# Front end of a fused attention and gated feed-forward kernel: four first projections split at once, value projections moved ahead, first scores in the first slot

## The chip, the cores and the metric

One core of one Trainium2 chip runs the whole program. The metric is the device time of one execution in microseconds (us); lower is better. TensorE (PE) does the matmuls, VectorE (DVE), ScalarE (ACT) and GpSimd (POOL) the elementwise work, and SyncE (SP) issues all the DMA transfers.

## What is computed

Input x is 2 x 1024 tokens of 512 features. The reference, cut to what matters:

```
xn = layernorm(x)                                   # over 512 features
q  = xn @ Wq            -> 32 heads of 16
kv = xn @ Wkv           -> 8 groups, a key and a value of 16 each (4 heads share a group)
w  = softmax(causal(q k^T) / 4);  ctx = w v;  s = ctx @ Wo + bo
gate, up = xn @ gate_w^T + lora,  xn @ up_w^T + lora        # 1376 hidden
g  = silu( (silu(gate) * up) @ down_w^T + lora )
out = x + s * g
```

## The kernel before

**Chunks.** The 2048 tokens are cut in four chunks `c` of 512. For each chunk the kernel normalises x (`layernorm`, DVE; its square root is `root`, ACT), transposes it on PE (`turn_x`, 4 turns a chunk, tile `ring` to a PSUM bank), rounds it (`round_x`, `x_hi`), copies it (`copy_x`, `xT`) and makes the rest (`low_x`, `x_lo`). Products in nearly full precision are three matmuls with high and low parts (L246 to L248). A projection `("proj", c, blk)` is 4 steps of three 512-column matmuls; block 4 (`KEYS_BLOCK`) makes the keys of all groups, blocks 0 to 3 make the queries of eight heads each. Its result is split in a high part on ACT (`split_projection`, L1125) and a low part on DVE (`low_projection`, L1374), and SP stores three pieces of it in DRAM (`store_projection`, L618, tiles `scratch_q` and `scratch_k`). A value `("value", c, 0)` is 4 steps of four 128-column matmuls (L896); ACT copies it (`copy_value`, L1132, tile `v_sb`, two buffers) and SP stores it (`store_value`, L623). The projections are counted by `projection(c, blk)`: 0 to 3 are `LEADING` (keys and block 0 of chunks 0 and 1), 4 is (0,1), 5 the keys of chunk 2, 6 is (1,1), 7 the keys of chunk 3.

**Two programs in one.** Each engine interleaves a background (all the projections, then the feed-forward) with the attention. `interleave` first runs `LEAD` steps of the background alone. Then it goes slot by slot: 40 slots are a round, round -1 comes first, then 16 rounds, one for each pair of a group and a batch. The `EARLY` steps are spread over round -1, and one background step falls to each slot of the rounds 0 to 15. PE, SP and POOL run their attention one slot further on than the others (`background_first` is false).

**Scores.** In round i the attention of pair i (scores transposed `st`, L1054; exponential, L1297; context, L1071) runs beside the maxima of pair i+1: 48 units, each a score matmul `s` (L1035, two units to a pair of matmuls) with a maximum on DVE (L1516 with the diagonal, L1519 without) through three PSUM banks. `stream_slots` spreads the pairs of units over the slots by their widths. The first 16 units of a pair need only the first 512 tokens, the other 32 all of them. SP loads q and k for them: for the first pair in two parts (`load_first`, L600 and L602, which waits at L598 until projections 0 and 1 lie in DRAM; then L790 and L793 at slot 1 of round -1, which wait at L785 for projections 2 and 3). For the second pair all comes at slot 1 of round 0 (again L790 and L793), after a wait at L785 until projections 6 and 7 lie in DRAM. PE's first score matmuls of the second pair stand in slot 6 of round 0; they are the 64x128 pair in front of the second turn of the maxima (L1042).

**The low-rank factors.** `split_low_b` (ACT, L1138) and `low_of_low` (DVE, L1380) prepare tile `bT`; `split_low_a` (L1144) and the same helper prepare `low_a`, which the first `fold` on PE needs. `low_a` lies where chunk data lay, so `split_low_a` waits until all four values are stored and landed.

Of the kernel before, what the change touches and what calls it, by code (L numbers as in the profile page):

```python
# [80 lines left out]
LOAD, LOAD_V = 1, 19  # L81
FIRST_UNIT, UNIT_SLOTS = 6, 39
CONTEXT = 2
COPY_O = [15, 3]
# [38 lines left out]
def bank_order():  # L123

    for c in range(2):
        for k in range(KT):
            yield "turn", c, k
    for c, blk in LEADING:
        yield "proj", c, blk
    for c in range(2):  # L130
        yield "value", c, 0
    for c in BESIDE:
        for k in range(KT):
            yield "turn", c, k
        yield ("proj", *BESIDE[c])
        yield "proj", c, KEYS_BLOCK
        yield "value", c, 0
    for c, blk in AFTER[:SOON]:
        yield "proj", c, blk
    for i in range(2):  # L140
        yield "fold", 0, i
    for h in range(NH):
        for c in range(NCH):
            yield "hidden", h, c
            if c == 1:
                if h + 1 < NH:
                    for i in range(2):
                        yield "fold", h + 1, i
                yield "proj", *AFTER[SOON + h]
    for h in range(NH):  # L150
        yield "down_fold", h, 0
    for t in range(NT):
        yield "down", t, 0
        if 1 <= t <= NT // 2:
            yield "out", t - 1, 0
    for t in range(NT // 2, NT):
        yield "out", t, 0
# [5 lines left out]
TOTAL = sum(STEPS[kind] for kind, *_ in NUMBER)  # L163
LEAD = sum(STEPS[kind] for (kind, *_), u in NUMBER.items() if u <= NUMBER["proj", 1, 0])
EARLY = NUMBER_STEPS["fold", 0, 1] - FIRST_HIDDEN - LEAD
# [54 lines left out]
def stream_slots():  # L220
# [5 lines left out]
    for kind, n in STREAM:  # L226
        if kind == "unit" and n % 2 == 0:
            g, w = divmod(n, NU)
            even = SLOTS * g + FIRST_UNIT + UNIT_SLOTS * sum(weight[:w]) // sum(weight)
            even -= even % 2  # L230
            slot = even if even > slot else even + 1
        slots.append(slot)
# [18 lines left out]
def layer(nc, x, Wq, Wkv, Wo, bo, gate_w, up_w, down_w, low_a, low_b, low_a_down, low_b_down, out):  # L251
# [5 lines left out]
    with ExitStack() as ctx:  # L257
# [329 lines left out]
        def _(sp):  # L587
# [106 lines left out]
            def background():  # L694
# [11 lines left out]
                for c in BESIDE:  # L706
                    yield KT * STEPS["turn"]
                    for n in range(4 * (c - 2), 4 * (c - 2) + 4):
                        load_raw(n)
                    yield STEPS["proj"]  # L710
                    store_projection(*BESIDE[c])
                    yield STEPS["proj"]
                    store_projection(c, KEYS_BLOCK)
                    yield STEPS["value"]
                    store_value(c)
                for c, blk in AFTER[:SOON]:
# [139 lines left out]
        def _(pe):  # L856
# [122 lines left out]
            def background():  # L979
# [8 lines left out]
                for c in BESIDE:  # L988
                    for kt in range(KT):
                        yield from turn_x(c, kt)  # L990
                    yield from project(*BESIDE[c])
                    yield from project(c, KEYS_BLOCK)
                    yield from value(c)
                for c, blk in AFTER[:SOON]:
# [102 lines left out]
        def _(act):  # L1097
# [42 lines left out]
            def split_low_a():  # L1140
                for i in range(2):
                    act.wait_ge(v_stored[i], DMA * NCH // 2)
                act.wait_ge(xn_ready, NCH)
                nc.scalar.activation(a_gu[:, :, :], a_raw, ACT.Copy).then_inc(low_hi, 1)  # L1144
# [8 lines left out]
            def split_weight(h, i):  # L1153
                key = ("fold", h, i)
                hp = rows[h]
                wait_filled(act, key)
                nc.scalar.activation(wh[:, h % 2, i, :, 0:hp],
# [42 lines left out]
            def background():  # L1200
# [14 lines left out]
                for c, blk in LEADING:  # L1215
                    if c == 1 and blk == KEYS_BLOCK:
                        root(3)
                        split_low_b()
                        for kt in range(KT):
                            copy_x(1, kt)  # L1220
                    yield STEPS["proj"]
                    split_projection(c, blk)
                for blk in range(1, NBLK - 1):
                    round_query_weights(blk)
# [3 lines left out]
                for c in BESIDE:  # L1228
                    for kt in range(KT):
                        yield STEPS["turn"]  # L1230
                        round_x(c, kt)
                        copy_x(c, kt)
                    yield STEPS["proj"]
                    split_projection(*BESIDE[c])
                    yield STEPS["proj"]
                    split_projection(c, KEYS_BLOCK)
                    yield STEPS["value"]
                    copy_value(c)
                split_low_a()
# [92 lines left out]
        def _(dve):  # L1332
# [108 lines left out]
            def background():  # L1441
# [7 lines left out]
                for c, blk in LEADING:  # L1449
                    yield STEPS["proj"]  # L1450
                    low_projection(c, blk)
                    if (c, blk) == (0, 0):
                        layernorm(3)
                low_of_low(0, bT, b_raw, slice(2 * BESIDE_ROWS, 3 * BESIDE_ROWS))
                yield 2 * STEPS["value"]
                for c in BESIDE:
                    yield KT * STEPS["turn"]
                    yield STEPS["proj"]
                    low_projection(*BESIDE[c])
                    yield STEPS["proj"]  # L1460
                    low_projection(c, KEYS_BLOCK)
                    yield STEPS["value"]
                low_of_low(1, a_gu, a_raw, slice(BESIDE_ROWS, 2 * BESIDE_ROWS))
# [127 lines left out]
```

## Time and profile before

| | us |
|---|---|
| time, median of three runs | 984.64 (982.81 to 989.12) |
| the profiled execution's own time | 989.02 |
| its span | 987.3 |
| PE busy | 927.0 (94% of the span) |
| DVE, ACT, POOL busy | 576.7, 487.5, 318.1 |
| PE's share of the chain that ended last | 84% |
| mean granted TensorE clock | 0.977 |

The page's chain of work that ended last is followed back from the last instruction; PE holds most of it, so a moment in which PE waits is a moment of the total. All that the change touches runs in the first 110 us of the span.

### The profile page before, as it was taken

The numbers are of one execution on the slowest core, as the hardware profiler recorded it, in microseconds if no ns is written. First come the engines' busy times: TensorE is split into PE (matmuls) and PEld (weight loads), VectorE is DVE, ScalarE is ACT, GpSimd is POOL, SyncE is SP. The second block draws the span as 40 slices with busy tenths as digits, with TensorE's granted clock in tenths as the row PEclk, the third lists the DMA queues.
The fourth block names the chain that finished last, engine by engine and source line by source line (L and its number), as shares of the span: only waits on it lengthen the run. The fifth ranks groups of instructions, "written<-read, shape, count | busy, mean of one in ns | idle before, by whom it ended". The sixth has DMA issues, their size and how long they took to land.

```text
span 987.3 us, 18068 instructions
## 1 busy us (share of the span) xinstructions
PE 927.0 (94%) x6599; PEld 598.5 (61%) x6599; DVE 576.7 (58%) x1659; ACT 487.5 (49%) x978; POOL 318.1 (32%) x320
## 2 busy tenths in 40 slices
PE   2797999999999999999999999999999999999986
PEld 2665667676766676767676766554555555555764
DVE  6755666666666666666666666676566656530025
ACT  2432556565656565656565656555444434435211
POOL 4022234343535352525252525330213122120126
PEclk9899999999999999999999999989999999999998
DMA  9456242424242424242424243367565454534454
GB/s 293 132 186 206 64 136 80 133 83 134 82 134 83 133 83 125 86 124 88 119 89 124 93 127 101 101 186 195 166 169 146 124 158 122 139 105 135 144 150 150
DMA packets 142934, 129.02 MB, mean 131 GB/s; under 512 B 36176, under 2 KB 104368, under 8 KB 142624
## 3 DMA queue, kind: packets, MB, share of 16 engines
q1 hardware_dynamic: 142848, 127.87, 43.6%
q8 instruction: 54, 0.88, 0.4%
q14 instruction: 32, 0.26, 0.1%
HBM read 74.07 MB, written 53.22 MB: 129 GB/s over the span
## 4 chain that ended last, share of the span: by engine, by line
PE 84%; DVE 8%; ACT 3%; DMA 2%; issue 2%; POOL 0%; SPq 0%; POOLq 0%; DVEq 0%; ACTq 0%
PE bank L934 24%; PE o L1071 12%; PE bank L246 9%; PE s L1035 9%; PE st L1054 9%; PE bank L247 7%; PE bank L248 7%; DVE junk L1516 2%; PE bank L896 2%; DVE neg_pad L1532 1%; PE bank L909 1%; PE bank L913 1%; DVE hid L1406 1%; DMA inv_sums<-scratch_r 1%; ACT gate L1168 1%
## 5 line engine op out<-in xcount | busy, mean ns | idle before, releaser
L1297 ACT ACTIVATE prob<-st 128x512 f32<-128x512 f32 (+1 forms) x640 | 324.3, 554 | 287.7 <-PE st L1054 287.1
L1516 DVE CUSTOM_DVE_ANT_0 junk<-s,mask 128x128 bf16<-128x128 f32 (+3 forms) x512 | 229.3, 487 | 116.3 <-PE s L1035 115.5
L1519 DVE TENSOR_REDUCE part_max<-s 128x1 f32<-128x512 f32 x256 | 163.8, 681 | 103.9 <-PE s L1035 103.7
L503 POOL TENSOR_SCALAR_AFFINE_SELECT prob<-prob 128x512 f32<-128x512 f32 x128 | 82.3, 655 | 262.1 <-ACT prob L1297 261.6
L1035 PE MATMUL s<-k,q 64*128 64x512 f32 (+3 forms) x768 | 150.0, 379 | 10.5 <-DVE part_max L1516 8.5
L934 PE MATMUL bank<-x_hi,w_hi 64*128 64x512 f32 (+1 forms) x704 | 150.9, 415 | 2.4 <-DVE hid L1406 1.1
L1071 PE MATMUL o<-prob,v 128*32 128x512 f32 (+3 forms) x1536 | 145.3, 497 | 0.0
L934 PE MATMUL bank<-x_lo,w_hi 64*128 64x512 f32 (+1 forms) x704 | 142.9, 391 | 0.0
L934 PE MATMUL bank<-x_hi,w_lo 64*128 64x512 f32 (+1 forms) x704 | 142.2, 389 | 0.0
L1054 PE MATMUL st<-q,k 64*128 64x512 f32 (+3 forms) x768 | 137.2, 375 | 3.9 <-ACT prob L1297 3.8
L512 POOL TENSOR_TENSOR tanh<-tanh,hid 128x512 f32<-128x512 f32 (+1 forms) x44 | 56.5, 1285 | 166.4 <-DVE hid L1406 166.4
L1035 PEld LDWEIGHTS s<-k,q 64*128 64x128 f32 x768 | 77.3, 186 | 52.6 <-DVE part_max L1516 28.3
L1054 PEld LDWEIGHTS st<-q,k 64*128 64x128 f32 x768 | 72.0, 185 | 59.6 <-issue 35.5
L934 PEld LDWEIGHTS bank<-x_hi,w_hi 64*128 64x128 f32 (+1 forms) x704 | 68.7, 182 | 41.3 <-issue 30.6
L246 PE MATMUL bank<-down_hi,hid_in 128*128 128x512 f32 (+1 forms) x176 | 79.2, 450 | 3.0 <-issue 2.3
L520 POOL TENSOR_TENSOR hid_lo<-hid,tanh_hid_hi 128x512 fp32r<-128x512 f32 (+1 forms) x44 | 56.7, 1288 | 75.9 <-ACT tanh_hid_hi L1185 75.9
L1071 PEld LDWEIGHTS o<-prob,v 128*32 128x32 f32 x1536 | 39.7, 110 | 66.2 <-issue 62.3
L934 PEld LDWEIGHTS bank<-x_lo,w_hi 64*128 64x128 f32 (+1 forms) x704 | 69.0, 182 | 12.6
L934 PEld LDWEIGHTS bank<-x_hi,w_lo 64*128 64x128 f32 (+1 forms) x704 | 69.1, 183 | 7.4
L247 PE MATMUL bank<-down_lo,hid_in 128*128 128x512 f32 (+1 forms) x176 | 70.1, 399 | 0.0
L248 PE MATMUL bank<-down_hi,hid_in 128*128 128x512 f32 (+1 forms) x176 | 69.9, 397 | 0.0
L514 POOL TENSOR_TENSOR hid<-tanh,hid 128x512 f32<-128x512 f32 (+1 forms) x44 | 56.5, 1283 | 3.5
(121 smaller groups left out, 1014.6 us busy)
## 6 DMA issues: line engine op xcount, KB each, us to landing
hid_in<-scratch_hid SPq DMA_DIRECT2D x16, 1408.0 KB, 7.4
q<-scratch_q SPq DMA_DIRECT2D x60, 200.0 KB
scratch_hid<-tanh_hid_hi SPq DMA_DIRECT2D x40, 256.0 KB, 2.1
scratch_hid<-hid_lo SPq DMA_DIRECT2D x40, 256.0 KB, 2.4
scratch_o<-o_sb SPq DMA_DIRECT2D x32, 256.0 KB
scratch_q<-proj_hi SPq DMA_DIRECT2D x30, 256.0 KB
k<-scratch_k SPq DMA_DIRECT2D x30, 192.0 KB
ctx<-scratch_o SPq DMA_DIRECT2D x16, 256.0 KB, 3.9
```

What stands on the lines that cost most here:

```text
L246: pe.matmul(out, lhs_hi, rhs_hi, start=start, stop=False)
L247: pe.matmul(out, lhs_hi, rhs_lo, start=False, stop=False)
L248: return pe.matmul(out, lhs_lo, rhs_hi, start=False, stop=stop)
L503: ins = pool.affine_select(out=blk, in_=blk, compare_op=ALU.is_ge, fill=0.0, base=0, pattern=[[0, REP], [1, P]], channel_multiplier=-1)
L520: pool.tensor_tensor(hid_l[0:hp, n % 2], hid[0:hp, n % 2], hid_h[0:hp, n % 2], ALU.subtract)\
L934: mm = pe.matmul(bank[i][0:hp, :], w_[half, h % 2, i, kt, 0:hp], x_[half, c, kt], start=not cross and kt == 0 and w_ is wh and x_ is xh, s ...
L1035: pe.matmul(sb_[(p + odd) % S_BANKS][:, 0:wd], q[half, g % 2, h // 2, qt * P:(qt + 1) * P], k[half, g % 2, k0:k0 + wd], start=True, stop=T ...
L1054: mm = pe.matmul(st[odd][:, col:col + q1 - q0], k[half, i % 2, kt * P:(kt + 1) * P], q[half, i % 2, h // 2, q0:q1], start=True, stop=True)
L1071: mm = pe.matmul(ob[32 * h:32 * h + 2 * HD, q0 % C:q0 % C + q1 - q0], v[:, i % 3, kt].rearrange("p a e -> p (a e)"), prob[:, job % 3, h, c ...
L1297: nc.scalar.activation(prob[:, job % 3, h, 0:JOB_COLS[j]], st[at % ST_BANKS][:, 0:JOB_COLS[j]], ACT.Exp, scale=float(HD) ** -0.5).then_inc ...
L1516: ins = dve.tensor_tensor_reduce(junk[:, n % S_BANKS, 0:wd], bank_[:, 0:wd], mask[:, C - wd:C], 1.0, LOWEST, ALU.add, ALU.max, part[:, h, ...
L1519: ins = dve.tensor_reduce(part[:, h, qt, dst:dst + 1], bank_[:, 0:wd], AX.X, ALU.max)
```

## The change

In the background's order, the value of chunks 2 and 3 is moved ahead of their projections. `LEAD` now ends after the values of chunks 0 and 1 (32 steps; 24 before), so `EARLY` has 34 steps (42 before). The units of the first pair are spread over 45 slots from slot 0 (before 39 slots from slot 6). ACT splits all four leading projections before it copies chunk 1's `xT`, and then does the square root of chunk 3 and `split_low_b`; on DVE the layernorm of chunk 3 stands behind the four low parts. The wait for the stored values moves from `split_low_a` to the first `split_weight`; `split_low_a` waits for POOL's last low part of x instead. Nothing is added or removed in the computation.

```diff
+FIRST_OF_ALL, FIRST_SLOTS = 0, 45
...
     for c in BESIDE:
         for k in range(KT):
             yield "turn", c, k
+        yield "value", c, 0
         yield ("proj", *BESIDE[c])
         yield "proj", c, KEYS_BLOCK
-        yield "value", c, 0
...
-LEAD = sum(STEPS[kind] for (kind, *_), u in NUMBER.items() if u <= NUMBER["proj", 1, 0])
+LEAD = sum(STEPS[kind] for (kind, *_), u in NUMBER.items() if u <= NUMBER["value", 1, 0])
...
-            even = SLOTS * g + FIRST_UNIT + UNIT_SLOTS * sum(weight[:w]) // sum(weight)
+            first, width = (FIRST_UNIT, UNIT_SLOTS) if g else (FIRST_OF_ALL, FIRST_SLOTS)
+            even = SLOTS * g + first + width * sum(weight[:w]) // sum(weight)
...
             def split_low_a():
-                for i in range(2):
-                    act.wait_ge(v_stored[i], DMA * NCH // 2)
-                act.wait_ge(xn_ready, NCH)
+                act.wait_ge(xT_lo_late, 2 * KT)
...
+                if h == 0 and i == 0:
+                    for odd in range(2):
+                        act.wait_ge(v_stored[odd], DMA * NCH // 2)
                 wait_filled(act, key)
...
                 for c, blk in LEADING:
-                    if c == 1 and blk == KEYS_BLOCK:
-                        root(3)
-                        split_low_b()
-                        for kt in range(KT):
-                            copy_x(1, kt)
                     yield STEPS["proj"]
                     split_projection(c, blk)
+                for kt in range(KT):
+                    copy_x(1, kt)
+                root(3)
+                split_low_b()
...
                     low_projection(c, blk)
-                    if (c, blk) == (0, 0):
-                        layernorm(3)
+                layernorm(3)
```

On SP, before the change, from the last load of raw feed-forward weights of round -1 to the loads of the second pair (line number, transfer, shape, count; `scratch_q` are the stores of projection 6, `scratch_k` those of projection 7, `scratch_v` the value of chunk 3, `k<-scratch_k` 48x1024 the first load for the second pair):

```order
L646 DMA ring<-in_L_ffn_up_w 128x512
L618 DMA scratch_q<-proj_hi 8x16x512 x2
L618 DMA scratch_q<-proj_lo 8x16x512
L618 DMA scratch_k<-proj_hi 8x16x512
L618 DMA scratch_k<-proj_lo 8x16x512
L618 DMA scratch_k<-proj_hi 8x16x512
L623 DMA scratch_v<-v_sb 128x8x64
L790 DMA k<-scratch_k 48x1024 x2
```

The same stretch of SP's queue after the change, with the line numbers of the new text:

```order
L648 DMA ring<-in_L_ffn_up_w 128x512
L625 DMA scratch_v<-v_sb 128x8x64
L620 DMA scratch_q<-proj_hi 8x16x512 x2
L620 DMA scratch_q<-proj_lo 8x16x512
L620 DMA scratch_k<-proj_hi 8x16x512
L620 DMA scratch_k<-proj_lo 8x16x512
L620 DMA scratch_k<-proj_hi 8x16x512
L792 DMA k<-scratch_k 48x1024 x2
```

The last value store has moved ahead of the stores of projection 6, so the loads for the second pair now stand directly behind the stores of projection 7. In the same way the two stores of the values of chunks 0 and 1, which stood behind the loads at L790 and L793 of round -1, now stand ahead of them.

On PE, the end of round -1 before the change (`x_hi,wk_lo` is the last matmul of projection 7, `wkv,xT` the value of chunk 3, `x_hi,wq_hi` the first step of the next projection, `s<-k,q` a pair of score matmuls of the first pair):

```order
L248 MATMUL bank<-x_hi,wk_lo 128x512
L1035 MATMUL s<-k,q 128x512 x2
L896 MATMUL bank<-wkv,xT 128x128 x8
L1035 MATMUL s<-k,q 128x256 x2
L896 MATMUL bank<-wkv,xT 128x128 x4
L1035 MATMUL s<-k,q 128x512 x2
L896 MATMUL bank<-wkv,xT 128x128 x4
L1035 MATMUL s<-k,q 128x384 x2
L246 MATMUL bank<-x_hi,wq_hi 128x512
```

And after it:

```order
L1037 MATMUL s<-k,q 128x512 x2
L248 MATMUL bank<-x_hi,wk_hi 128x512
L249 MATMUL bank<-x_lo,wk_hi 128x512
L250 MATMUL bank<-x_hi,wk_lo 128x512
L248 MATMUL bank<-x_hi,wq_hi 128x512
L249 MATMUL bank<-x_lo,wq_hi 128x512
L250 MATMUL bank<-x_hi,wq_lo 128x512
L1037 MATMUL s<-k,q 128x384 x2
```

Before, the four steps of chunk 3's value stood between the end of projection 7 and the 384-column pair; now projection 7 ends one step ahead of that pair, and is the work whose end comes last.

## Rows read from the trace of the kernel before

**Rows 1.** Chain that ended last, 82 to 97 us: start, duration, what
```profile
87.38 1.11 PE bank L896 x8
...
88.51 0.61 ACT v_sb L1132
...
89.14 4.30 DMA scratch_v<-v_sb
...
93.51 1.07 ACT low_a L1144
...
94.60 1.22 DVE low_a L1380
...
96.56 0.80 PE s L1035 x2
```

**Rows 2.** Waits of PE, 0 to 110 us: us in total, times, longest
```profile
PE s L1035 <- DVE part_max L1516: 6.0, 2, 5.7
...
PE bank L896 <- DVE prob L1374: 4.8, 1, 4.8
```

**Rows 3.** By stretch: length, PE, PEld, DVE, ACT, POOL busy, granted clock, DMA share, GB/s
```profile
43.80:52.00 8.20, 8.17 (x58) 8.08 (x58) 4.35 (x2) 1.79 (x4) 1.27 (x1) 0.79 0.40 116
...
96.60:104.60 8.00, 7.75 (x36) 5.28 (x38) 4.62 (x13) 4.01 (x8) 0.63 (x1) 0.67 0.36 97
```

**Rows 4.** Timeline, 20 to 60 us, of DVE: start, us, line, operation, tiles
```profile
34.84 2.46 DVE L1345 BATCH_NORM_STATS2 stats<-ring 128x6 f32<-128x512 f32 x4
...
39.27 1.92 DVE L1359 TENSOR_SCALAR ring<-ring,mean_var,small 128x512 f32<-128x512 f32 x4
...
44.31 3.88 DVE L1380 TENSOR_TENSOR bT<-prob,bT 32x2752 fp32r<-32x2752 f32 x1
```

**Rows 5.** Timeline of PE, 60 to 84 and 103.5 to 106 us
```profile
67.97 2.94 PE L896 MATMUL bank<-wkv,xT 128*128 128x128 f32 x24
...
82.75 0.39 PE L248 MATMUL bank<-x_hi,wk_lo 128*128 128x512 f32 x1
...
104.61 0.27 PE L1035 MATMUL s<-k,q 64*128 64x128 f32 x2
```

**Rows 6.** Timeline of SP's queue, 20 to 125 us
```profile
44.58 1.69 SPq L600 DMA_DIRECT2D k<-scratch_k  x2
...
59.21 0.78 SPq L790 DMA_DIRECT2D k<-scratch_k  x2
...
85.75 0.64 SPq L618 DMA_DIRECT2D scratch_k<-proj_hi  x1
89.14 0.39 SPq L623 DMA_DIRECT2D scratch_v<-v_sb  x1
92.61 1.08 SPq L790 DMA_DIRECT2D k<-scratch_k  x2
```

**Rows 7.** Waits of SP's queue, 0 to 130 us: us in total, times, longest
```profile
SPq L598 <- DMA scratch_q<-proj_lo: 6.4, 1, 6.4
SPq L785 <- DMA scratch_q<-prob: 5.0, 1, 5.0
```

**Rows 8.** Timeline of the weight loads: the first pair over all tokens
```profile
63.09 0.19 PEld L1035 LDWEIGHTS s<-k,q 64*128 64x128 f32 x2 [0.36 <-DMA q<-scratch_q]
```

**Rows 9.** Chain that ended last, 44 to 70 us: a pair, a turn, a matmul
```profile
54.22 0.44 PE s L1035 x2
54.66 0.59 PE bank L867 x4
...
58.20 0.23 PE bank L247
```

**Rows 10.** By stretch, columns as rows 3: the DMA ahead of and at the loads
```profile
54.00:58.20 4.20, 3.69 (x22) 2.36 (x21) 3.19 (x16) 3.75 (x8) 2.81 (x3) 1.00 0.51 197
58.20:60.00 1.80, 1.80 (x10) 0.89 (x8) 0.78 (x4) 0.56 (x2) 1.80 (x2) 1.00 0.04 15
...
99.00:100.00 1.00, 1.00 (x3) 0.39 (x2) 0.00 (x0) 0.00 (x0) 0.00 (x0) 0.50 0.46 143
100.00:101.00 1.00, 1.00 (x5) 0.50 (x4) 0.13 (x1) 0.63 (x2) 0.00 (x0) 0.50 0.03 12
```

More of the change, by code:

```diff
@@ L709, in background @@
                         load_raw(n)
+                    yield STEPS["value"]
+                    store_value(c)
                     yield STEPS["proj"]
@@ L713, in background @@
                     store_projection(c, KEYS_BLOCK)
-                    yield STEPS["value"]
-                    store_value(c)
                 for c, blk in AFTER[:SOON]:
@@ L990, in background @@
                         yield from turn_x(c, kt)
+                    yield from value(c)
                     yield from project(*BESIDE[c])
                     yield from project(c, KEYS_BLOCK)
-                    yield from value(c)
                 for c, blk in AFTER[:SOON]:
@@ L1232, in background @@
                         copy_x(c, kt)
+                    yield STEPS["value"]
+                    copy_value(c)
                     yield STEPS["proj"]
@@ L1236, in background @@
                     split_projection(c, KEYS_BLOCK)
-                    yield STEPS["value"]
-                    copy_value(c)
                 split_low_a()
@@ L1456, in background @@
                 for c in BESIDE:
-                    yield KT * STEPS["turn"]
+                    yield KT * STEPS["turn"] + STEPS["value"]
                     yield STEPS["proj"]
@@ L1461, in background @@
                     low_projection(c, KEYS_BLOCK)
-                    yield STEPS["value"]
                 low_of_low(1, a_gu, a_raw, slice(BESIDE_ROWS, 2 * BESIDE_ROWS))
```

## The prediction

> **What bounds the kernel now.** I read the chain of waits first. PE holds 84% of it, so a microsecond in which PE stands is one of the total, and work moved about on a busy PE is worth nothing. Then PE's waits in the first 110 us, where all of the change lies. Two are touched. One is 4.8 us, from 39 to 43.8, ahead of the first value matmul [rows 2]. The other is 5.7 us, from 90.9 to 96.6, and the chain shows what fills it: the copy of chunk 3's value, 4.30 us for its store to land, 1.07 us for ACT's rounding of `low_a`, 1.22 us for DVE's part, one maximum, and only then a free score bank [rows 1]. The table by stretch shows that PE pays for each idle spell a second time: behind them the mean granted clock is 0.79 over 8.2 us and 0.67 over 8.0 us [rows 3], which is the lower level (1.2 instead of 2.4 GHz) for 3.4 and 5.3 us. Half of that time is lost: 1.7 and 2.6 us. Last I read SP's queue and its waits, since scores cannot begin before q and k have been to DRAM and back.
>
> The most to be had is thus 4.8 + 5.7 + 1.7 + 2.6 = 14.8 us. I expect nearly none of it to stay, because in both places a transfer that the change does not speed up stands right behind the removed wait.
>
> **First part: the wait of 4.8 us.** ACT now splits projections 2 and 3 as they come, DVE makes their low parts by about 40.4, and PE goes on to the values at 39. The 64 value matmuls take 0.12 us each at full clock (24 in 2.94 us, [rows 5]), 7.8 us, so they end at 46.8. What is late next:
>
> - The first loads of q and k. SP issues them at 44.58, 6.4 us after the last store of projection 1 [rows 6, 7], and none of this moves. The nearest duration is the 3.9 us from the issue at 59.21 to the pair that those loads released at 63.09 [rows 6, 8], so they are there at about 49.
> - DVE. It now does the layernorm of chunk 3 behind all four low parts. From 40.4, with 6.4 us for the layernorm (34.84 to 41.2) and 3.88 us for `bT` [rows 4], the first maximum comes at 50.7. The first score matmuls were at about 51.9.
>
> So score work starts over 1 us earlier with 8 value matmuls (1 us) fewer to come and a turn done. But the next gate takes this back. The pairs over all 1024 tokens need the loads at L790, which wait for the stores of projections 2 and 3: last one issued at 54.2, landed 5.0 us later, at 59.2 [rows 6, 7]. SP's queue is the same up to there. Before, the first such pair began at 63.09, its weight load released by that load of q [rows 8]: the load had just made it. In the new order PE reaches this pair after 43 background steps, before after 41. From the second pair on, at 51.1, its way there is the old one of 11.2 us with three value steps (+1.5 us) more and two projection steps (-1.4 us, three matmuls of 0.23 us each), a turn (-0.6) and a pair (-0.4) fewer [rows 9]. That gives 61.4, and PE waits until 63.1. This part is worth 0 at that point. What is left to the background's 64th step then has two projection steps more (1.4 us) and four value steps fewer (1.9 us): 0.5 us less. The 64th step ended at 88.49 [rows 1]; now it is the end of projection 7, which I call T. T = 88.5 - 0.5 = 88.0.
>
> The two value stores that now stand ahead of the L790 loads I cost at nothing: while the projections' stores run, the DMA engines are busy 0.51 of the time at 197 GB/s, and from 58.2 to 60.0 they are at 0.04 [rows 10], so 0.5 MB fits in. Should it not, the bound above is the 4.3 us in which one value store landed [rows 1]. The Trainium skill (DMA: Bandwidth & Descriptors, section on queues, rings and completion order) says that each DMA engine consumes descriptors in ring order. By that rule the loads queue behind the value stores, which speaks against this change; no row shows this case yet. By it the sum would be up to 4.3 us higher.
>
> **Second part: the wait of 5.7 us.** The value of chunk 3 is stored 8 steps earlier, and its landing gates nothing. From T: ACT splits projection 7 (0.6 us, as its copy of a value) and rounds `low_a` in 1.07 us, until T+1.8; DVE needs 1.22 us, to T+3.0, and 0.7 us for the maximum that frees a bank (94.60+1.22 to 96.56, [rows 1]). PE comes for that bank at T+2.4 and gets it at T+3.7, so 1.3 us of wait stay of 5.7: -4.4 us. From there to the 64x128 pair in slot 6 of round 0 PE needed 8.05 us (96.56 to 104.61), 5.3 of them at the lower clock; at full clock 5.4. It arrives at T+9.1 = 97.1. If nothing else waited, this would be -7.5 us.
>
> But that pair needs the loads for the second pair of group and batch, and they wait for the stores of projection 7. Before, projection 7 ended at 83.1 [rows 5] and four value steps stood behind it; now nothing does. Its last store was issued until 86.4, 3.3 us later [rows 6]: T+3.3. Landing after the last issue took 6.4 us, 5.0 us [rows 7] and here 6.2 us (86.4 to 92.61, [rows 6]); I take 6.2, the same store behind the same neighbour: T+9.5. SP then issues at once. The data of these loads ran from the issue at 92.61 to 100 [rows 6, 10], 7.4 us, for all six transfers; the pair needs four of them, and the smaller loads took 3.9 us. I take 5.5, near the middle. So the pair starts at T+15.0 = 103.0, with bounds T+12.2 (5.0 and 3.9) and T+17.1 (6.4 and 7.4). Against 104.61: -1.6 us, and PE stands 5.9 us in front of it. That is as long as the stall removed, so I expect the same fall of the clock behind it: +2.0 us, between the 1.7 and the 2.6 of the two spells there are. The 2.6 us of the old stall lie inside the 104.61 already.
>
> **Sum.** -1.6 + 2.0 = +0.4 us; behind slot 6 the order is the old one. The profiled execution (989.02) stands 4.4 us above the median, so I put the difference on the median: 984.6 + 0.4 = 985.0.
>
> **Rivals.**
>
> - The new stall is short. At the lower bound the pair comes at T+12.2 = 100.2, 4.4 us earlier, after 3.1 us of idle time, and the clock may stay up. That gives 980.2. For it speaks that the stores of projection 7 no longer follow raw weights closely. Chance 0.17.
> - The loads gate nothing and the change does what it says: -7.5 us, 977.1. Store and load together would have to take 5.8 us from the last issue, where the shortest rows give 8.9. Chance 0.04.
> - Slower: the value stores go ahead of the L790 loads on the rings and delay the first pair over all tokens. At 1.6 us more than hidden this decides against the kernel; with 3 to 4.3 us, and 1.7 us for a clock that falls because PE then waits over 4 us there, everything after moves back: up to 991, 989 in the middle. Against it stands the idle DMA time [rows 10]. Chance 0.13.
> - The sum above, 985.0, with its own range 981.5 to 988.5: chance 0.61. The rest, 0.05, is for effects in the rounds that I don't see.
>
> The range goes from the first rival less 1.7 us, the spread of the runs below their median, to the slower case's middle plus 1: 978.5 to 990. About 1% is what a measurement of this kernel can tell from no change; that is 974.8 or 994.5, beyond every case but combinations. Faster 0.04, same 0.93, slower 0.03.
>
> **What would show it.** In the trace of the changed kernel: PE goes straight from the leading projections to the values at 39; the first maximum comes near 50.7; the loads for all tokens are issued at 59 and the first pair over them starts at 63 (over 1 us later: the value stores are in the way). The landing of chunk 3's value is gone from the chain, and SP's wait for `scratch_k<-proj_hi` is about 6. PE stands 5 to 6 us ahead of the 64x128 pair at about 103, released by `q<-scratch_q`, with a lower clock behind it. If PE walks through slot 6 without a wait, or the stores land within 3 us of the last issue, the prediction is wrong by up to 7.5 us.

## The result, and the profile after

| | before | changed |
|---|---|---|
| time, median of twelve runs | 986.33 us (982.81 to 990.52) | 991.46 us (988.97 to 996.89) |
| ratio, with its 95% interval | | 1.0054 (1.0033 to 1.0075) |
| the profiled execution's own time | 989.02 | 989.31 |
| its span | 987.3 | 987.6 |
| PE busy | 927.0 | 922.2 |
| mean granted TensorE clock | 0.977 | 0.984 |

The change costs 5.1 us, half a per cent. That is within 1%, as predicted, but the median lies 1.5 us above the upper end of the predicted range. The two profiled executions are of almost the same length: that of before is a long one of its kernel, that of the changed kernel a short one. So the whole spans say nothing here, and what follows compares places inside them.

The range was put on the median of three runs of before, 984.6 us; over twelve it is 986.3. These 1.7 us alone are more than the 1.5 us by which the range is missed. What was wrong whatever the base is the difference: +0.4 us forecast, +5.1 us measured.

**The second gate.** These are pieces of the chain of waits of the changed kernel, from the end of projection 7 to slot 6 of round 0 (start, duration, what). They answer to [rows 1].

```profile
90.39 0.24 PE bank L250
90.66 0.61 ACT proj_hi L1127
91.29 0.70 DVE proj_lo L1376
92.01 0.57 SPq L620
92.63 0.56 SPq L620
93.23 6.02 DMA scratch_k<-proj_hi
99.32 0.34 SPq L792
...
100.87 4.77 DMA q<-scratch_q
105.69 0.47 PE s L1037 x2
```

The landing of chunk 3's value is gone from the chain. In its place stand the store of the last keys, 6.02 us from its issue, and the load behind it, 4.77 us. The form is that of the prediction; T, the end of projection 7, is 90.6 instead of 88.0. These are the longest of PE's waits from 38 to 125 us (us in total, times, longest); in [rows 2] 4.8 and 5.7 us stood there.

```profile
PE s L1037 <- DMA q<-scratch_q: 7.6, 2, 5.5
PE s L1037 <- DVE part_max L1516: 4.0, 4, 1.4
PE bank L898 <- ACT xT L1114: 2.1, 2, 1.2
PE s L1037 <- DVE part_max L1519: 1.2, 2, 0.8
PE bank L869 <- ACT xT L1114: 0.5, 1, 0.5
```

The wait of 5.5 us for q was forecast (5.9). The row for `xT` was not: PE waits ahead of both moved values until ACT has copied the last quarter of the chunk's `xT`. Before, two projections stood in between and covered that copy.

**The front.** This is the timeline of the changed kernel from 38 us on (start, duration, engine, line, what, with the idle time before it and its releaser).

```profile
38.30 7.30 PE L898 MATMUL bank<-wkv,xT 128*128 128x128 f32 x64
47.74 0.36 PE L1037 MATMUL s<-k,q 64*128 64x128 f32 x2 [2.13 <-DMA q<-scratch_q]
50.22 0.29 DVE L1516 CUSTOM_DVE_ANT_0 junk<-s,mask 128x128 bf16<-128x128 f32 x1
50.58 0.58 PE L1037 MATMUL s<-k,q 64*128 64x256 f32 x2 [1.44 <-DVE part_max L1516]
...
56.01 2.05 PE L898 MATMUL bank<-wkv,xT 128*128 128x128 f32 x16 [0.85 <-ACT xT L1114]
...
64.36 0.49 PE L1037 MATMUL s<-k,q 64*128 64x512 f32 x2
```

And this is the table by stretch (from:to, length, then busy time and instructions of PE, of its weight loads, DVE, ACT and POOL, granted clock, DMA share, GB/s). It answers to [rows 3].

```profile
45.60:47.70 2.10, 0.01 (x1) 0.00 (x0) 2.07 (x3) 2.10 (x5) 1.27 (x1) 1.00 0.65 200
47.70:54.70 7.00, 5.53 (x24) 3.81 (x24) 4.83 (x13) 3.24 (x7) 2.55 (x2) 0.51 0.50 175
54.70:64.40 9.70, 8.37 (x54) 6.22 (x53) 5.13 (x21) 1.86 (x4) 3.72 (x3) 1.00 0.80 228
64.40:90.60 26.20, 22.30 (x116) 15.00 (x116) 15.58 (x44) 6.79 (x13) 6.22 (x5) 1.00 0.51 152
100.20:105.70 5.50, 0.01 (x2) 0.01 (x2) 0.64 (x1) 0.60 (x1) 0.00 (x0) 0.71 0.75 195
105.70:109.50 3.80, 3.80 (x17) 1.61 (x19) 0.51 (x4) 0.74 (x2) 1.23 (x2) 0.52 0.64 210
```

The wait of 4.8 us is gone from 39 us and comes back as 2.1 us for q and 1.4 us for a score bank. Behind them the clock is at its lower level for nearly 7 us. From 64.4 us to the end of projection 7 PE works 22.3 of 26.2 us; in the kernel before it worked 24.7 of the 25.5 us from 63 to 88.5.

**A spell that comes and goes.** A spell is a stretch at the lower clock here. The trace of before, from which all rows ahead of the prediction are read, has one from 20 to 30 us. A second trace of the same kernel (below, "Both kernels once more") hasn't; these are their rows of that stretch, before first.

```profile
20.00:30.00 10.00, 7.86 (x26) 6.63 (x27) 9.33 (x23) 4.55 (x9) 0.00 (x0) 0.50 0.77 278
```

```profile
20.00:30.00 10.00, 7.85 (x34) 6.74 (x35) 9.21 (x22) 5.04 (x10) 0.00 (x0) 1.00 0.76 269
```

With the spell the first value matmul of before starts at 43.83, without it at 42.52, and the pair of slot 6 at 104.61 and 103.27. All three traces of the changed kernel are without it; there the values start at 38.3 to 38.5 us, and in the variants of it whose trace has the spell at 38.7 to 39.6. So places of a trace with the spell are to be compared with such a trace alone, or 0.4 to 1.3 us are put down to the wrong cause. It is in the traces of before, the late values, the front alone, the first pair later, the value between, the keys ahead, the raw loads and the short store, and in no other.

### The profile page after: what moved, and what is told of

It is laid out like the page before. It is cut to its first block, busy times and chain, and to the rows that moved or that the text cites. A ratio compares the mean times of both kernels' runs of the same rounds, so it can differ in the third digit from the quotient of the medians.

```text
span 987.6 us, 18068 instructions
## 1 busy us (share of the span) xinstructions
PE 922.2 (93%) x6599; PEld 595.0 (60%) x6599; DVE 577.1 (58%) x1659; ACT 487.3 (49%) x978; POOL 318.7 (32%) x320
## 4 chain that ended last, share of the span: by engine, by line
PE 83%; DVE 9%; ACT 3%; DMA 2%; issue 2%; SPq 0%; POOL 0%; POOLq 0%; DVEq 0%; ACTq 0%
PE bank L936 24%; PE o L1073 12%; PE bank L248 9%; PE s L1037 9%; PE st L1056 9%; PE bank L250 7%; PE bank L249 7%; DVE junk L1516 2%; DVE neg_pad L1532 1%; PE bank L911 1%; PE bank L915 1%; DVE hid L1408 1%; PE bank L898 1%; ACT gate L1171 1%; DVE ring L1361 1%
## 5 line engine op out<-in xcount | busy, mean ns | idle before, releaser
L1037 PEld LDWEIGHTS s<-k,q 64*128 64x128 f32 x768 | 77.3, 186 | 60.6 <-DVE part_max L1516 26.3
```

The costliest lines, as they stand in the source:

```text
L1037: pe.matmul(sb_[(p + odd) % S_BANKS][:, 0:wd], q[half, g % 2, h // 2, qt * P:(qt + 1) * P], k[half, g % 2, k0:k0 + wd], start=True, stop=T ...
```

## The experiments

Each kernel is timed against the kernel before on the same chip; the median of before was 985.4 us in the first two batches and 986.0 in the third. Two theories stood against each other for the 2.6 us by which T is late: **A**, the first maxima are denser and PE pays in score banks and in the clock; **B**, the values ahead of their projections wait for `xT`.

### The late values alone

The kernel before, with two of the changes: the values of chunks 2 and 3 ahead of their projections, and the wait for stored values moved out of `split_low_a`.

```diff
+        yield "value", c, 0
         yield ("proj", *BESIDE[c])
         yield "proj", c, KEYS_BLOCK
-        yield "value", c, 0
...
             def split_low_a():
-                for i in range(2):
-                    act.wait_ge(v_stored[i], DMA * NCH // 2)
-                act.wait_ge(xn_ready, NCH)
+                act.wait_ge(xT_lo_late, 2 * KT)
```

> The kernel before with only the second part of the change: the values of chunks 2 and 3 ahead of their projections, and low_a no longer waiting for stored values. Theory A (the loads for the second pair of group and batch gate slot 6 of round 0, 15 us after the end of projection 7): projection 7 ends at 88.0 to 88.5, PE stands 5 to 6 us ahead of the first 64x128 pair of slot 6 and starts it at about 103.3, against 104.6 before, and loses 1.9 us behind it at the lower clock: +0.6 us, between -1 and +2. Rival B (the removed wait is a gain, only the front of the change costs): no wait over 1 us in front of that pair, -7 us.

Measured: 992.43 us, ratio 1.0060 (1.0038 to 1.0083). This part by itself costs as much as the whole change. PE's waits from 50 to 100 us and from 70 to 130 us, and two lines of its timeline:

```profile
PE bank L896 <- ACT xT L1112: 2.3, 2, 1.2
...
77.97 2.05 PE L896 MATMUL bank<-wkv,xT 128*128 128x128 f32 x16 [1.11 <-ACT xT L1112]
...
PE s L1035 <- DMA q<-scratch_q: 6.5, 1, 6.5
...
107.04 0.48 PE L1035 MATMUL s<-k,q 64*128 64x128 f32 x2 [6.53 <-DMA q<-scratch_q]
```

The keys end at 91.0 with the old front, so theory A is not needed for a late T; the wait for `xT` is there in the same size. This trace and that of before both have the spell at 20 us. The pair of slot 6 starts 16.1 us behind the keys.

### The front alone

The changed kernel, with the late values behind their projections and the old wait in `split_low_a`: the reverse of the diff above.

> The changed kernel with only the first part: four leading projections split at once, values 0 and 1 ahead of the attention, first scores in slot 0; values of chunks 2 and 3 behind their projections and low_a waiting for the stored values as before. Theory A (the changed front costs 2.6 us of position by the 64th background step: idle PE at 45.6 to 50.6, a lower clock until 54.7, PE and DVE taking turns): the 64th step ends at about 91 instead of 88.5, the 5.7 us wait for the value store stays, slot 6 at about 107.2: +2.6 us. Rival B (the front is neutral and what the changed kernel lost comes from the late chunks): 0 us. Rival C (the front is a gain as it was meant): -4 us.

Measured: 985.24 us, ratio 0.9996 (0.9981 to 1.0010), where +2.6 us was expected. The pair of slot 6 starts at 105.02, and the old wait for stored values is there as before (PE's waits from 70 to 130 us):

```profile
PE s L1037 <- DVE part_max L1516: 5.7, 1, 5.7
```

So splitting four projections at once, values earlier and scores from slot 0 are worth nothing together, neither gain nor loss, when nothing else is changed. Theory A falls as the main cause: the 64th background step ends at 89.45 here, 1.0 us later than the 88.49 of before (both with the spell at 20 us), where 91 was expected.

### The moved wait alone

The kernel before, with nothing but the wait moved: the `split_low_a` part of the diff above, and

```diff
             def split_weight(h, i):
...
+                if h == 0 and i == 0:
+                    for odd in range(2):
+                        act.wait_ge(v_stored[odd], DMA * NCH // 2)
```

> The kernel before with one thing changed: low_a is rounded without waiting for the stored values (they are waited for at the first split weight). Theory A: the loads for the second pair still go out at 92.6, since nothing ahead of them moves; the wait of 5.7 us shrinks to about 1.3, PE reaches slot 6 at about 97.5 and waits there only 1 us for the loads that land at 98.5: slot 6 at 98.7 instead of 104.6, no lower clock, -6 us. Rival B (whatever is taken away in front of slot 6 comes back as a wait for the loads): 0 to -1 us.

Measured: 982.90 us, ratio 0.9963 (0.9946 to 0.9980): 2.5 us faster than before, and 8.6 us below the changed kernel's median. Two of its chain's pieces, then PE's waits from 70 to 130 us:

```profile
85.51 7.42 DMA scratch_k<-proj_hi
...
94.53 4.70 DMA q<-scratch_q
99.28 0.47 PE s L1035 x2
...
PE s L1035 <- DMA q<-scratch_q: 1.7, 1, 1.7
```

The pair of slot 6 starts at 99.28, 5.3 us earlier than in [rows 5] and 4.0 us earlier than in the second trace of before, which like this one is without the spell at 20 us; 1.7 us of wait are left. The place comes near the 98.7 expected, the gain does not reach the 6 us expected. Those were counted against the slot 6 of a late trace and without a lower clock, of which 3.4 us follow here (0.83 from 95 to 105). Laid beside each other by the exponentials on ACT (640 of them, in the same order in every kernel), this trace is 3.7 and 2.5 us ahead of the two traces of before, 3.1 in the mean, and the medians show 2.5. The values behind the projections are the cover: PE makes them while the keys go to DRAM and back. In the order of the change these steps stand in front of T, and the same round trip is bare.

### The first pair later

The changed kernel with `FIRST_OF_ALL, FIRST_SLOTS = 6, 39`, as the first pair was spread before.

> The changed kernel with the first pair's units back in slots 6 to 45. Theory A (scores in slot 0 make PE stand for the loads and DVE while background steps were there to be done, and this brings the lower clock): no idle spell over 1.5 us and no lower clock between 39 and 60, first scores at about 51, projection 7 ends at 86 to 87 instead of 90.6, slot 6 still 15 us later at about 101.5 to 102; 3 to 4 us faster than the changed kernel, that is about 0 to +2 against before. Rival B (the first pair over all tokens sets the pace whatever is in front of it): as the changed kernel, +4 to +5 against before.

Measured: 988.86 us, ratio 1.0038 (1.0020 to 1.0055). The keys still end at 90.8 (the values start 0.4 us late, behind the spell at 20 us), where 86 to 87 was expected, and the wait for `xT` (2.0 us) stays. The clock is at its lower level here too, 0.51 from 50 to 57 us. Against the changed kernel's median this is 2.6 us less; in the trace the exponentials come 1.1 us earlier than in the changed kernel's first. The intervals of the two ratios overlap, and I count nothing for it.

### The value between the two projections

```diff
         yield ("proj", *BESIDE[c])
+        yield "value", c, 0
         yield "proj", c, KEYS_BLOCK
```

> The changed kernel with the values of chunks 2 and 3 between their two projections: the projection that uses only chunk 0 or 1 stands behind the turns again, so that PE does not come to the value before ACT has copied the turned x. Theory A2 (in the changed kernel PE waits 1.2 us twice for the last copies of xT, hidden before by that projection, and this is what made projection 7 end late): no wait of L898 for xT, projection 7 ends at about 88.3 instead of 90.6, slot 6 still 15 us later at 103.4; 2.3 us faster than the changed kernel. Rival B (the changed front makes projection 7 late): as the changed kernel.

Measured: 987.44 us, ratio 1.0009 (0.9990 to 1.0028), 4.0 us below the changed kernel. The two intervals of the ratios do not overlap. No value waits for `xT` any more. The keys end at 90.0, not at the 88.3 expected, but this trace has the spell at 20 us and the changed kernel's hasn't. These are its rows, then the changed kernel's, then the start of its second pair, which in the changed kernel is at 50.58:

```profile
20.00:30.00 10.00, 6.87 (x24) 5.82 (x25) 9.67 (x21) 4.42 (x9) 0.00 (x0) 0.51 0.69 258
47.00:58.00 11.00, 7.05 (x28) 4.84 (x29) 8.01 (x17) 6.50 (x13) 5.45 (x5) 0.69 0.57 187
```

```profile
20.00:30.00 10.00, 7.84 (x35) 6.86 (x36) 9.45 (x24) 5.05 (x10) 0.00 (x0) 1.00 0.74 271
47.00:58.00 11.00, 7.98 (x42) 5.82 (x42) 6.84 (x17) 5.21 (x11) 5.80 (x6) 0.69 0.62 198
```

```profile
51.87 0.58 PE L1037 MATMUL s<-k,q 64*128 64x256 f32 x2 [1.66 <-DVE part_max L1517]
```

Up to that pair the two kernels do the same work in the same order, and this one is 1.3 us late there. From it to the end of the keys it takes 38.1 us, the changed kernel 40.05 (50.58 to 90.63): 1.9 us less, where 2.3 were expected and 2.1 us of waits for `xT` are gone. The lower level behind the first scores lasts equally long in both (0.69 over 11 us). So theory B holds, in nearly the size expected. The pair of slot 6 comes at 104.82 behind a wait of 5.3 us: still the bare round trip.

### The keys ahead of the queries

```diff
-PROJECTED = LEADING + [p for c in BESIDE for p in (BESIDE[c], (c, KEYS_BLOCK))] + AFTER
+PROJECTED = LEADING + [p for c in BESIDE for p in ((c, KEYS_BLOCK), BESIDE[c])] + AFTER
...
         yield "value", c, 0
-        yield ("proj", *BESIDE[c])
         yield "proj", c, KEYS_BLOCK
+        yield ("proj", *BESIDE[c])
```

> The changed kernel with the keys of chunk 3 (and 2) projected ahead of the query block beside them: the last store that the loads for the second pair wait for is that of the keys, so these are stored four steps earlier, and the query block's store no longer counts. Theory A (stores of the keys of chunk 3, then the loads, gate slot 6): the keys end at about 86.3, the loads go out at about 95.8 instead of 99.3, the first pair of slot 6 starts at about 101.5 instead of 105.7, after a wait of 1 to 2 us and with little or no lower clock behind it: 4 to 6 us faster than the changed kernel, that is -1 to +1 against before. Rival B (the DMA is the limit, or something else waits at slot 6): as the changed kernel, +5.

Measured: 989.59 us, ratio 1.0037 (1.0016 to 1.0058). The keys end at 86.5, 4.1 us earlier, and the pair of slot 6 starts at 105.50 instead of the 101.5 expected. From its chain:

```profile
94.47 0.56 SPq L620
...
95.16 1.20 SPq L792
97.86 7.59 DMA q<-scratch_q
105.50 0.47 PE s L1037 x2
```

The keys had landed in time, and SP waits for nothing (the second pair of this trace, too, is 1.2 us late, behind the spell at 20 us). But SP's queue holds three stores of query block (1,1) ahead of the loads, the last issued at 94.47. The loads are issued behind them at once, and the last of them then takes 7.59 us instead of 4.77; from the first issue to the pair it is 10.3 us instead of 6.4. The round trip did not get shorter; its waiting moved from the semaphore to the transfers. This is what the prediction weighed for another place: the Trainium skill (DMA: Bandwidth & Descriptors, section on queues, rings and completion order) has each DMA engine consume descriptors in ring order, and this trace agrees, with 2.8 us more for a load behind 0.75 MB of stores. Whether it is the order, or only that stores and loads share the engines, these rows don't tell apart.

### Raw loads moved out of the way

The kernel with the moved wait alone, and the raw loads 4 to 7 issued behind the store of chunk 3's keys instead of ahead of it, so that the stores have the DMA engines for themselves.

```diff
                 for c in BESIDE:
                     yield KT * STEPS["turn"]
-                    for n in range(4 * (c - 2), 4 * (c - 2) + 4):
-                        load_raw(n)
+                    if c == 2:
+                        for n in range(4):
+                            load_raw(n)
...
                     store_projection(c, KEYS_BLOCK)
+                    if c == 3:
+                        for n in range(4, 8):
+                            load_raw(n)
```

> The run with only the wait of low_a moved (982.9 us), with the four raw weight loads of chunk 3 issued behind the stores of its keys instead of ahead of them. Theory A (what is left in front of slot 6 is the time of the keys' store behind 1 MB of raw weights): the loads for the second pair go out at 92.2 instead of 93.0, slot 6 at 98.4 instead of 99.3, the wait of 1.7 us shrinks to about 1: -0.5 to -2 us against that run, the more if the lower clock behind slot 6 goes too. Rival B (the stores run on other engines' time and do not feel the raw loads): 0.

Measured: 986.59 us, ratio 1.0007 (0.9987 to 1.0026), 3.7 us worse than without this edit. SP's queue and PE's timeline:

```profile
92.90 1.08 SPq L794 DMA_DIRECT2D k<-scratch_k  x2
...
100.95 0.33 PE L1039 MATMUL s<-k,q 64*128 64x128 f32 x2 [1.80 <-DMA q<-scratch_q]
```

The stores land no earlier (loads issued at 92.90, against 93.00), and the pair starts 8.05 us behind that, against 6.28 us, behind 1 MB of raw loads issued from 85.89 to 90.46 (DMA share 0.89 from 90 to 95 us, against 0.57). The expectation failed for the same reason as the one before. The edit has a second effect. The store of chunk 3's value stands behind the raw loads, too (issued at 90.51 instead of 88.73), and the moved wait, in front of the first `split_weight`, now holds ACT until 97.02:

```profile
97.02 0.60 ACT L1162 ACTIVATE w_hi<-bank 128x512 fp32r<-128x512 f32 x1 [1.74 <-DMA scratch_v<-v_sb]
```

PE waits 1.8 us for the exponential behind it and reaches slot 6 late by 1.5 us, too. The loads are still the last to come, so the pair's 1.7 us are theirs. The other 2 us of the medians stay open.

### The front with the moved wait

The changed kernel with the values behind their projections, but the wait moved.

> The changed kernel with the values of chunks 2 and 3 behind their projections as before; that is the changed front and the moved wait of low_a together. Theory A (front alone 0, wait alone about -3 us, and slot 6 hangs on the keys of chunk 3, which end at 83.5 in both): slot 6 at about 99.5, -3 us against before, as the moved wait alone. Rival C (the front is a gain that only shows when the wait behind it is gone): -6 us. Rival D (the front was hidden by that wait and costs when it is gone): 0 us.

Measured: 981.23 us, ratio 0.9959 (0.9936 to 0.9982). The keys end at 83.8, the pair of slot 6 starts at 100.39 behind a wait of 1.0 us. Together with the run of the moved wait alone it says: the gain is that of the wait, and the front adds nothing that can be told (the two intervals overlap; in the two traces, both without the spell at 20 us, this kernel's slot 6 is 1.1 us later). Both kernels are faster than before and than the changed one.

### A short store of the last keys

The changed kernel, with each store of chunk 3's keys cut to an eighth; seven of eight columns of these keys are left out, and what stands there instead is stored earlier (behind projection 4). The result is wrong by that, the work of the engines is the same.

```diff
                 for j, part_ in enumerate(parts):
-                    sp.dma_start(dst[:, j], part_).then_inc(p_stored[n % 2], DMA)
+                    cut = C // 8 if n == 7 else C
+                    sp.dma_start(dst[:, j, :, 0:cut], part_[:, 0:cut]).then_inc(p_stored[n % 2], DMA)
```

> The changed kernel, with the three stores of projection 7 (the keys of chunk 3) cut to an eighth of their columns, 32 KB each; the region is filled earlier, behind the store of projection 4, from x_hi, so the keys of chunk 3 are wrong in it for 7 of 8 columns. All the arithmetic is done as before, only the bytes of this store are gone from where they gate. Theory A (these stores and then the loads gate slot 6): SP's wait at L787 falls from 6 us to 2 to 3, the loads go out at about 96 instead of 99.3, slot 6 starts at about 102 instead of 105.7 after 2 us of waiting; 3 to 5 us faster than the changed kernel. Rival B (the rings are busy with the stores of projection 6 anyway, or the loads themselves are slower): slot 6 not before 105, 0 to 1 us faster.

Measured: 987.62 us, ratio 1.0014 (0.9987 to 1.0041), 3.8 us below the changed kernel, though the two intervals overlap a little. SP's wait, its loads, PE's last matmul of projection 7 and the pair of slot 6:

```profile
SPq L794 <- DMA scratch_k<-proj_hi: 1.3, 1, 1.3
...
98.34 0.81 SPq L799 DMA_DIRECT2D k<-scratch_k  x2
...
92.89 0.40 PE L250 MATMUL bank<-x_hi,wk_lo 128*128 128x512 f32 x1
...
104.32 0.33 PE L1044 MATMUL s<-k,q 64*128 64x128 f32 x2 [1.48 <-DMA q<-scratch_q]
```

T is 93.3 here, so the loads go out at 98.3 and not at the 96 expected. Of the 2.7 us 2.6 are there before the edit does anything: the first pair over all tokens starts at 66.97 instead of 64.36, and the stores that fill the region are issued at 72.75. The values start 0.7 us later, behind the spell at 20 us, and the lower clock behind the first scores lasts 10.1 us (0.54 from 50 to 61) instead of 6.9. From T to the pair are 11.0 us instead of 15.0, and SP waits 1.3 instead of 5.5 us. So it is the landing of these stores that holds slot 6. The lower clock at slot 6 lasts 3.4 us here (0.66 from 105 to 110) instead of 6.8.

### Both kernels once more

Two more profiled executions of the changed kernel and one of the kernel before, to see what varies from one execution to the next.

> The changed kernel once more, for a second trace. The traces so far put it 2.8 us behind the kernel before from slot 8 of round 0 to the end of the attention, the times 5.1 us. Theory T (the rest is in spells of the lower clock that differ from run to run): positions up to slot 6 repeat within 0.5 us, and the difference of this trace to the first is where low spells are. Rival: a wait in some later round that the first trace did not have.

> The kernel before once more, for a second trace. Theory T: slot 6 at 104.6 within 0.5 us; its first trace had a low spell of 10.2 us at 658, near the end of the attention, where the changed kernel had 6.8; if such spells are chance, this one has another length, worth half of it, and the kernel's own time (989.0 then, 986.3 in the median) goes with it.

> The changed kernel a third time, for a third trace; the same expectation as for the second.

Measured: 992.20 and 989.97 us for the changed kernel, 983.46 for the kernel before. In the changed kernel the pair of slot 6 starts at 106.64 and 106.16 behind waits of 6.2 and 5.7 us, where the first trace had 105.69; in before once more it starts at 103.27. Neither repeats within the 0.5 us expected. In before the spell at 20 us accounts for the difference as far as the values (1.3 us); in the changed kernel T is 90.6, 90.9 and 90.9, and the rest lies behind it. Laid beside the first trace of before, the exponentials of the rounds run later by 2.75, 3.6 and 3.2 us in the three traces of the changed kernel, and 1.3 us earlier in the second trace of before. The means are 3.2 and -0.65, so the front end costs 3.8 us. The rest varies, most clearly near 658 us, where the change moves nothing. Of the stretch from 640 to 690 us these are the rows of before, of before once more, and of the changed kernel:

```profile
640.00:690.00 50.00, 46.72 (x302) 25.45 (x299) 36.18 (x99) 29.19 (x60) 11.81 (x14) 0.90 0.64 183
```

```profile
640.00:690.00 50.00, 46.02 (x313) 25.77 (x311) 36.98 (x104) 30.20 (x63) 10.72 (x13) 1.00 0.67 189
```

```profile
640.00:690.00 50.00, 45.53 (x307) 25.10 (x307) 37.26 (x101) 31.09 (x64) 12.61 (x14) 0.93 0.59 167
```

One program had a clock of 0.90 there in one execution and of 1.00 in the next, which is 10.2 us at the lower level or none. Ahead of it the exponentials of before once more are 1.2 us earlier than those of the first trace, behind it 4.4 us: this spell cost 3.2 us and not half of its length; why not half stays open. This is why a single profiled execution could not show a difference of 0.5%.

## Why the prediction was wrong, point by point

**The step that failed is T.** The prediction had it as "88.5 - 0.5 = 88.0"; it is 90.6. Two errors of different sign are in it: one term had the wrong size, and the waits and the clock of the front were left out.

*The term.* The prediction took 0.5 us for a step of a value ("three value steps (+1.5 us) more", "four value steps fewer (1.9 us)"). Of PE's instructions by line and shape, this is the row of before from 63 to 88.5 us and that of the changed kernel from 64.3 to 90.65 us (count, then busy time, mean ns, idle time before them):

```profile
L896 PE MATMUL bank<-wkv,xT 128*128 128x128 f32 x64 | 8.4, 281 | 0.0
```

```profile
L898 PE MATMUL bank<-wkv,xT 128*128 128x128 f32 x32 | 4.4, 285 | 1.2 <-ACT xT L1114 1.2
```

The first holds both late values, eight steps in 64 instructions of the trace. So a step is eight of them, twice the four that the code writes, and at 24 in 2.94 us [rows 5] it takes 0.98 us. The prediction had used just this for the 7.8 us of the leading values and half of it afterwards.

*What that changes.* PE's way to the first pair over all tokens becomes 1.4 us longer, 62.8 instead of 61.4, still ahead of the 63.1 at which the prediction let a load release it. Behind it four value steps fewer are 3.9 us, so T would have been 63.1 + 25.4 - 3.9 + 1.4 = 86.0. Against that sum the trace is 4.6 us late, not 2.6, and all of it is what the prediction did not price:

- *Up to 64.36, 1.3 us.* The second pair starts at 50.58. The way of 11.2 us, with 2.9 us for three value steps and less the other terms, leads to 62.3. Waits are 0.85 us for `xT` and 0.48 us for a score bank, 1.1 us more than the 0.26 us in the old way. And until 54.7 the clock is lower: a pair with two turns took 2.5 us (52.13 to 54.64), where pairs and turns at the full clock would need some 1.7, so by this estimate 1.2 us are lost from 50.58 on. That makes 64.6, and 64.36 was measured. The prediction saw PE done with the leading values at 46.8 and the loads there at 49, and yet priced no clock for the idle time between. The load was not the gate that it had been; it was issued at 57.85 and PE came late by itself.
- *From there to T, 26.3 us instead of 22.9.* PE waits 3.8 us (1.2 for `xT`, 2.1 for score banks, 0.5 for a turn's bank), and before it waited 0.7 us from 63 to 91. That is 3.1 of the 3.4 us.

The run of the late values alone puts a size on the part of the order in this. Up to T it makes the same 64 steps as the kernel before, and T is 91.0 against 88.5: 2.5 us, of which 2.3 us stand in its waits for `xT`. The value between the projections gives 1.9 us of this back.

The 88.5 is itself a number of the trace with the spell at 20 us. In the second trace of before the same step ends at 87.4, and T of the changed kernel is 90.6, 90.9 and 90.9. So against both traces of before the change makes T later by 2.8 us in the mean, where the prediction had it 0.5 us earlier.

**What held.** From T the form of the sum was right: 15.0 us to the pair of slot 6 predicted, 15.05 in the first trace, 15.75 and 15.3 in the two others. That the first agrees to a tenth is luck: the landing came 5.5 us behind SP's last store issue (93.8) for 6.2, and the load's way took 6.4 us (99.32 to 105.69) for 5.5. PE stood 5.5 us for 5.9. The wait for a score bank ahead of it, 1.3 us predicted, is 1.2 us at 94.2. The lower clock lasts 6.8 us, of which 3.2 lie in the wait (0.71 over 5.5 us) and 3.6 behind it (0.52 over 3.8 us of busy PE): 1.8 us lost, 2.0 predicted. The short store and the moved wait show the same gate from two sides. The old wait for stored values is gone, as said. The maxima begin at 50.22 (50.7 predicted).

**The sum again.** With T later by 2.6 us the sum of the prediction becomes 0.4 + 2.6 = 3.0 us. The traces show 3.8 at the exponentials, the medians 5.1. The 0.8 lie in the comparison of traces: slot 6 of before is at 104.61 in the trace that the sum was made against, the one with the spell at 20 us, and at 103.27 in the other, so that trace was a late one by 0.7 us against their mean. The last 1.3 us stay open: they are less than the 3.2 us that the spell near 658 us gives or takes, and no run separates them from chance.

**The rivals.** The slower one named the value stores ahead of the L790 loads, by the ring order of the Trainium skill. The price came out near (989 in its middle) by luck, since the mechanism did not come: the loads were issued at 57.85, earlier than predicted, and the first pair over all tokens was not waiting for them. In two other places, the keys ahead of the queries and the raw loads moved, loads behind other transfers of SP came 1.8 to 2.8 us later, so such a price exists, and the place was wrong. The short new stall (980.2) didn't come: the pair came at T+15.05, not at T+12.2. "The change does what it says" didn't either, and the run of the moved wait shows where it would have: with the values left where they were.

**Why no gain.** The change contains one edit that is worth 2.5 us by itself, the moved wait, and one that takes it back with interest, the values ahead of the projections. By the ratios, the moved values added to the moved wait cost some 9.5 us, with the old front (1.0060 against 0.9963) as with the new (1.0054 against 0.9959). The values moved without the wait were not run. In the order before, the values of chunk 3 did two things: they delayed `low_a` and they covered the keys' round trip through DRAM. The change ended the first twice over (by the moved wait and by the new order) and the second altogether.

## What to carry to other kernels

A step that seems to sit in front of a stall may be what hides the next gate: before moving it forward, count from the gate's own start (here the end of the keys) how long its round trip is, 14.8 to 16.6 us here where nothing else stood in its way, and what work is left to cover it. When two edits remove the same wait, take the one that moves no work. And when a step is moved, price what it reads: the copy that two projections used to cover cost 1 us each time it was bare.

## What the runs showed of the hardware

- A load came later when it was issued right behind other traffic of the same queue, though SP waited for nothing: the last load of q took 4.7 to 4.8 us where no store stood close ahead and 7.59 us behind 0.75 MB of stores. Behind 1 MB of raw loads the first use came 8.05 instead of 6.28 us after the issue.
- How long PE idled does not by itself tell how long the lower clock lasts. Idle times of 2.1 and 1.4 us were followed by 6.9 us of it, 5.5 us by 6.8 us (3.2 of them still in the wait), 1.7 us in front of slot 6 (the moved wait alone) and 1.5 us (the short store) by 3.4 us, but 1.0 us in front of slot 6 (the front with the moved wait) again by 6.8 us (0.52 from 100 to 105, 0.80 from 105 to 110).
- The same program had the lower clock for 10.2 us near 658 us in one execution and not at all in another, and likewise from 20 to 30 us, with the same waits of PE ahead of it (12.4 and 4.8 us for x). The first was worth 3.2 us at the exponentials behind it, the second 1.3 us at the first values.
